# Masked row maximum with the half maxima in SBUF and eleven feed-forward blocks, in a two-stage attention kernel

## What is computed

```python
# attention stage: 16 heads of 16 channels
q = (x @ Wq.T + bq).reshape(B, S, H, D)          # k and v likewise, v with its bias bv
scores = einsum('bqnd,bknd->bnqk', q, k) / sqrt(D)
attn = softmax(scores, axis=1)                    # over the 16 heads n
out = einsum('bnqk,bknd->bqnd', attn, v)
return out.reshape(B, S, E) @ Wo.T + bo           # then x + this, layer norm
# layer stage, twice: window attention (8 heads of 64), then
h = layernorm(shift_token(x)) @ w1 + b1           # w1: 256 x 1364, HID = 682
a, g = split(h, 2, axis=-1)
x = x + (a * gelu(g)) @ w2 + b2                   # w2: 682 x 256
```

## Time and profile before

| | before |
|---|---|
| median of 3 runs | 4322.89 us (4319.83 to 4324.39) |
| the profiled execution | 4329.71 us, its span 4327.9 us |
| attention stage (first to last L409) | 63.6 to 1482.5 us of the span |
| layer stage (from the first projection) | about 1525 to 4328 us |
| PE, DVE, ACT, POOL busy | 92%, 71%, 66%, 51% of the span |
| DMA queues | under 20% of 16 engines |

### The profile page before, as it was taken

How to read it: one execution, slowest core, us unless ns; L and a number is a source line. 1 busy time by engine, 2 the same in 40 slices (tenths; PEclk the granted TensorE clock), 3 DMA queues, 4 the chain that set the end, 5 groups by cost and what they waited for, 6 DMA issues and landing times.

```text
span 4327.9 us, 96690 instructions
## 1 busy us (share of the span) xinstructions
PE 4001.2 (92%) x36356; PEld 3306.8 (76%) x36416; DVE 3055.6 (71%) x7412; ACT 2852.8 (66%) x7273; POOL 2198.8 (51%) x2168
## 2 busy tenths in 40 slices
PE   5999999999999769999999999999999999999997
PEld 3777777777777557888888888877888888888886
DVE  3888888888888756666666666666667666666664
ACT  3666666666666456677676767766766676666665
POOL 3888888988888823333333333333333333333332
PEclk8999999999999989999999999999999999999999
DMA  5453444434444010000000000000000000000000
GB/s 103 69 74 63 60 69 70 68 63 66 68 70 59 28 45 12 20 16 16 19 17 14 17 19 16 16 27 13 26 21 21 27 21 21 22 26 24 19 24 24
DMA packets 175047, 159.22 MB, mean 37 GB/s; under 512 B 22175, under 2 KB 173558, under 8 KB 174582
## 3 DMA queue, kind: packets, MB, share of 16 engines
q1 hardware_dynamic: 174582, 153.04, 19.1%
HBM read 52.31 MB, written 25.17 MB: 18 GB/s over the span
## 4 chain that ended last, share of the span: by engine, by line
PE 16%; issue 15%; ACT 15%; DVE 14%; POOL 5%; SPq 0%; DMA 0%; POOLq 0%; DVEq 0%; ACTq 0%
PE b_X L1439 4%; PE b_S L1459 3%; DVE b_S L1251 3%; PE b_M L1561 3%; ACT b_p L1199 3%; ACT b_hn L1083 2%; ACT L1167 2%; PE b_M L1552 2%; DVE b_ss L1225 2%; DVE b_qT L1240 2%; ACT b_g L1167 2%; DVE b_kT L1240 2%; POOL b_rstd L1041 1%; PE b_F L1588 1%; PE b_S L1469 1%
## 5 line engine op out<-in xcount | busy, mean ns | idle before, releaser
L251 POOL TENSOR_TENSOR a_z<-a_p 128x1024 f32<-128x1024 f32 x256 | 604.0, 2359 | 187.4 <-ACT a_p L338 184.9
L1199 ACT ACTIVATE b_p<-b_S,b_nb 128x256 f32<-128x256 f32 (+1 forms) x1024 | 444.5, 446 | 328.8 <-DVE b_nb L1251 328.8
L338 ACT ACTIVATE a_p<-a_S 128x512 f32<-128x512 f32 x1024 | 528.7, 602 | 191.3 <-PE a_S L528 189.5
L1439 PE MATMUL b_X<-b_wqkv,b_hT 128*128 128x512 f32 x2304 | 651.5, 419 | 1.3 <-DVE b_hT L1275 1.3
L1508 PE MATMUL b_F<-b_hnT,b_w 128*114 128x256 f32 (+1 forms) x4608 | 628.8, 286 | 5.7 <-issue 5.7
L1508 PEld LDWEIGHTS b_F<-b_hnT,b_w 128*114 128x114 f32 (+1 forms) x4608 | 573.6, 177 | 19.0 <-issue 6.1
L1439 PEld LDWEIGHTS b_X<-b_wqkv,b_hT 128*128 128x128 f32 x2304 | 418.1, 190 | 101.2 <-issue 21.8
L977 POOL TENSOR_TENSOR b_t<-b_t 128x512 f32<-128x512 f32 x128 | 165.1, 1290 | 633.8 <-DVE b_t L1223 633.8
L422 DVE TENSOR_TENSOR a_p<-a_p,a_O 128x1536 f32<-128x1536 f32 x256 | 447.2, 1747 | 5.4 <-ACT a_O L315 3.8
L1588 PE MATMUL b_F<-w_w,b_a 114*128 114x256 f32 (+1 forms) x1536 | 365.4, 388 | 69.4 <-DVE b_a L879 68.8
L1260 DVE TENSOR_SCALAR b_a<-b_F,w_b 114x256 f32<-114x256 f32 (+1 forms) x384 | 183.8, 479 | 340.9 <-ACT b_g L1110 340.8
(11 more groups left out here) (152 smaller groups left out, 8719.7 us busy)
## 6 DMA issues: line engine op xcount, KB each, us to landing
a_q<-a_parts SPq DMA_DIRECT2D x256, 128.0 KB, 5.0
a_k<-a_parts SPq DMA_DIRECT2D x256, 128.0 KB, 5.0
a_x<-in_x SPq DMA_DIRECT2D x16, 512.0 KB, 3.9
a_xr<-in_x SPq DMA_DIRECT2D x64, 128.0 KB, 5.2
x_after_heads<-a_n SPq DMA_DIRECT2D x64, 128.0 KB, 5.4
b_x<-x_after_heads SPq DMA_DIRECT2D x16, 512.0 KB, 4.1
x_after_layer<-b_xo SPq DMA_DIRECT2D x32, 256.0 KB, 2.8
b_x<-x_after_layer SPq DMA_DIRECT2D x16, 512.0 KB, 4.1
```

What stands on the lines that cost most here:

```text
L251: nc.gpsimd.tensor_tensor(z8[:], e[:, 0:8], e[:, 8:16], ALU.add).then_inc(s_zt, 1)
L338: nc.scalar.activation(probs[u % NE][:, hs], S[:, hs], ACT.Exp, scale=HDIM ** -0.5).then_inc(s_exp, 1)
L1199: last = nc.scalar.activation(probs[hf][:, i, keys(w_)], SB[:, i, keys(w_)], ACT.Exp, bias=nb[hf][:, i:i + 1], scale=-1.0, accum_out=rs[w_ ...
L1439: last = nc.tensor.matmul(X[i][:], hT_of(k, a), wqkv[:, b, k, i * INNER:(i + 1) * INNER], start=(k == 0 and (a, b) == PART_PAIRS[0]), stop ...
```

## The change

In the attention stage:

- The second half maximum goes to SBUF, into `half_max[:, 1]` beside the first, instead of `HM` in PSUM. Its waits for `s_lz` and `s_Y` are gone. The minimum now has both its inputs in SBUF.
- The first part of `sum_z` stands before bank 0 instead of before bank 1, and `output` after `times_v` and its neighbours instead of before.
- V's bias comes from a matmul of three bf16 rows into the bank (one of 512 columns for each two tiles), and V is moved to SBUF by ScalarE with plain copies at the end of units 14 and 15, instead of by VectorE.

In the layer stage:

- Chunks are 128 columns wide, five full and one of 42. The last chunk's value and gate columns stand in one block of 106 (values in columns 0 to 41, gates from 64), so there are 11 blocks, 66 matmuls in a pair of tiles.
- w2 and b2 come from the host as one array padded with zero rows to 6 x 128, in one DMA instead of three; all six L1588 chunks take 128 rows. The scale rows `srow` share the memory of `t2[0]`.

The diff's core:

```diff
-    Z, HM = YZ[:, 1, :P], YZ[:, 1, P:]
+    Z = YZ[:, 1, :P]
...
-                    nc.vector.tensor_reduce(out=low_max[:], in_=S[:, 0:8].rearrange("p h q -> p q h"),
-                                            axis=AX.X, op=ALU.max, negate=True).then_inc(s_hm, 1)
...
-                    if exists(nz):
-                        dve.wait_ge(s_lz, UNITS * nz + uz + 1)
-                    ny, _, uy = lagged(n, u, 5, UNITS)
-                    if uy % TILES == TILES - 1 and exists(ny):
-                        dve.wait_ge(s_Y, TILES * ny + uy // TILES + 1)
-                    dve.wait_ge(s_S, 2 * U + 2)
-                    nc.vector.tensor_reduce(out=HM, in_=S[:, 8:16].rearrange("p h q -> p q h"),
-                                            axis=AX.X, op=ALU.max, negate=True).then_inc(s_hm, 1)
+                    for half in range(2):
+                        dve.wait_ge(s_S, 2 * U + half + 1)
+                        nc.vector.tensor_reduce(out=half_max[:, half], in_=S[:, 8 * half:8 * half + 8].rearrange("p h q -> p q h"),
+                                                axis=AX.X, op=ALU.max, negate=True).then_inc(s_hm, 1)
                     dve.wait_ge(s_hm, 2 * U + 2)
                     need(dve, s_sub, 4 * U - 4)
-                    nc.vector.tensor_tensor(negmax[u % 2][:], low_max[:], HM, ALU.min).then_inc(s_nm, 1)
+                    nc.vector.tensor_tensor(negmax[u % 2][:], half_max[:, 0], half_max[:, 1], ALU.min).then_inc(s_nm, 1)
...
+                nc.tensor.matmul(B[j][:].rearrange("p (t c) -> p t c", t=2), ones_b[:],
+                                 b_rows[:, VALUE].unsqueeze(1).to_broadcast([3, 2, CH]), start=True, stop=False,
+                                 skip_group_check=True)
...
-            size = HC if c < CHUNKS - 1 else LAST
-            for part in range(2):
+            size = HC if c < CHUNKS - 1 else GATE_AT + LAST
+            for part in range(2 if c < CHUNKS - 1 else 1):
                 for k in range(CT):
-                    col = part * HID + c * HC
+                    col = part * FULL + c * HC if c < CHUNKS - 1 else 2 * FULL
```

More of the change, by code:

```diff
@@ L321, in _ @@
             part_of_qk(0, i, part)
+        act.wait_ge(s_pz, 3)
+        for j in range(2):
+            evacuate_v(0, 0, j)
         def normalise_rows(nn, qt):
@@ L575, in _ @@
                 project_v(0, tile, k)
-        pe.wait_ge(s_bor, 16 * 3)
         for b in range(4):
```

107 lines of the change are left out of this document (56 added, 51 removed).

## The result

The changed kernel takes 4288.26 us (median of 4 runs, 4285.34 to 4290.59) against 4323.08 (4319.83 to 4324.39) for the kernel before: a ratio of 0.992, with a 95% interval of 0.9903 to 0.9937. That is 35 us, or 0.8%, faster, where I had said 4304 and a range of 4258 to 4328.

The account below looks back on a forecast made before the run. It took attention's loop to close over exps, z8 and minimum, and layer tiles over a chain on engines other than TensorE. Terms 42 - 19 - 4.5 + 0 + 1, about 19 us, took the 4322.9 us median to 4304, range 4258 to 4328.

Parts of the forecast that it names:

- The wait for the output: Attention, output units: VectorE's second reduce no longer waits for the output projection; 0.65 us in each of 64, 42 us gained.
- The first sum moved: Attention: first sum of z ahead of bank 0 starts bank 1 0.12 to 0.22 us sooner, but counts nothing.
- the gain is swallowed whole: Attention: the moved sum's gain is lost because the minimum must wait for z8, which does not move.
- The lock term of 19 us: Attention: the minimum waits for GpSimd's z8 at the SBUF port; 0.11 us in each of 11 ordinary units, 19 us lost.
- z4 first: Attention: GpSimd's z4 precedes the minimum every time, 1.5 us a unit, about 4550 us; within the GpSimd-pace rival, chance 0.12.
- The minimum with two SBUF inputs: Attention: it waits for z8 and ends some 0.15 us after it, 0.4 to 0.8 us long; 19 us lost in all.
- The rival of no lock: Attention: port does not matter for so short an instruction; 26 us gained instead of 19 lost, 4259 us; chance 0.10.
- V's bias and move: Attention, units 12 and 14: two more matmuls per sequence, 0.3 us on the path, 4.5 us lost; ScalarE's copies cost nothing.
- The feed-forward blocks: Layer stage: six matmuls fewer save TensorE 0.70 us a pair, but it only waits longer before the scores; 0 us.
- one wait of 1.05: Layer stage, odd tiles: TensorE's wait before the scores grows from 0.35 to about 1.05 us.
- The loads: Ahead of the layer stage's first x: two DMA issues fewer, 1 us gained.
- The sum: Whole kernel: 42 - 19 - 4.5 + 0 + 1, about 19 us gained, median 4304 us, 0.44% faster.

Follow-up runs that it names:

- experiment 4: Changed kernel with the first sum of z back behind bank 0's scores, as before the change: 4331.45 us, ratio 1.0024 to the kernel before.
- experiment 5: Kernel of experiment 4 with one added wait: in unit 8 GpSimd's z4 waits for VectorE's minimum: 4315.76 us, ratio 0.9983 to the kernel before.
- experiment 1: Changed kernel with the minimum as a tensor_reduce over half_max, one SBUF input instead of two: 4256.02 us, ratio 0.9848 to the kernel before.
- experiments 1, 2 and 5: The second of these: kernel before with only both half maxima moved to SBUF, waits and order kept: 4371.59 us, ratio 1.0113.
- experiment 8: Changed kernel with twelve feed-forward blocks, the last chunk's second block of 106 columns and its gate read from partitions 64 to 105: 4293.85 us, ratio 0.9934.
- Experiment 10: Changed kernel with the second weights loaded in three transfers (114 partitions, 14 partitions, sixth block) instead of one of 128: 4296.7 us, ratio 0.9938.

## Why the prediction came out as it did

*The wait for the output.* Right in kind, its size too small. I gave an output unit 5.75 us (5.5 in unit 15), and it took 5.43 to 5.45: by the medians a sequence gains 3.84 us, not 2.7, and the kernel 61 us, not 42. The terms of the sum were too long. From `less_max` to the less-part, with both sums and all scores between, I had 1.86 + 1.26 = 3.12 us, and it is 2.96 (879.63 to 882.59); the output is 1.15, not 1.18. For `times_v` I took the middle of 1.01 and 1.24, and it took 1.01 (882.90 to 883.91). That is 0.16 + 0.03 + 0.13 (with the rounding up to 5.75), the whole difference of 0.32. The times from the earlier trace rows had switches between sums and scores in them, and that these go away when the first sum stands ahead of all scores is my reading; the late weights of the upper end did not come. My 42 us was also 2 us off my own terms: 25.5 - 22.75 is 2.75 us in a sequence, 44 in all.

*The first sum moved, "the gain is swallowed whole".* True of nine of the eleven ordinary units, which are 5.37 to 5.47 us without it and 5.37 to 5.45 with it (experiment 4). False of the kernel: the move is worth 43 us where I had none, and without it the changed kernel would take 4331 us, 8 more than the kernel before. This is the step that failed. The lock term of 19 us holds only while the minimum starts ahead of z4. I priced the rival "z4 first" as one that strikes all units or none, and gave it its chance on the evidence of one pair of rows; what decides it is who starts first, in each unit anew, and in unit 8 GpSimd comes 0.23 us behind the minimum with the sum moved, and 0.08 ahead of it without. That one unit is worth 16 us (experiment 5) to 23. So that the forecast's sign came out is in part luck: it hung on a part of the change that I had put at nothing.

*The minimum with two SBUF inputs.* Right: 0.65 us at the median, its end 0.15 us after z8's, ordinary units at 5.36 to 5.39 us. They lose 1.45 us in a sequence, 23 us in all, where I had 1.2 and 19. The rival of no lock fell with experiment 1; against a minimum with one SBUF input the lock costs 32 us, and that with a minimum that is 0.14 us slower by itself.

The Trainium skill's page "SBUF — State Buffer", section "Who interferes with whom", on which a sentence of the prediction drew, has the rule of experiments 1, 2 and 5: two SBUF inputs contend with a GpSimd instruction that reads SBUF, one doesn't, and whoever starts first holds the port for its whole instruction. The runs agree (0.42 us without exception with one input; 0.29 with two and z4 held back; 1.33 with z4 first).

*V's bias and move.* Unit 14 is 0.12 us longer, 2 us in all, and unit 13 is with the ordinary ones, 0.22 longer; I had 4.5 us for both, within its bounds of 0 to 9.

*The feed-forward blocks.* Right that the matmuls bring nothing, and for the reason given. From the second weights' matmuls behind the odd tile to the next scores I count 7.75 us in the earlier trace rows (3018.55 to 3026.30), and now 8.56 (2973.53 to 2982.09):

```profile
2973.53 2.75 PE L1582 MATMUL b_F<-w_w,b_a 128*128 128x256 f32 x12
...
2980.20 0.44 PE L1416 MATMUL b_X<-c_ident,b_hn 128*128 128x128 f32 x2 [0.32 <-ACT b_hn L1077]
...
2982.09 0.98 PE L1454 MATMUL b_S<-b_kT,b_qT 64*128 64x256 f32 x12 [0.43 <-DVE b_kT L1235]
```

Those 0.81 us are the 0.70 saved and 0.11 on top. They don't stand in one wait of 1.05, as I had written, but in a new one for the layer norm, in a longer one for the key copy and in small gaps between. The 0.11 is what I missed: the gate is now read from partitions 64 to 105, VectorE's wait for it went from 2.86 to 2.98, and the stage lost some 8 us (2711.4 to 2719.6 by the means of experiment 8) where I had 0.

*The loads.* I allowed 1 us for two issues fewer. The stretch between the stages takes 47.6 to 49.5 us in the three traces with transfers of 114 partitions against 43.1 to 44.5 in the eleven without, 4.5 us by the means. The first `less_max` comes at 62.4 to 63.9 us against 57.5 to 62.8, 3 us by the means, but the two ranges overlap, so that this part is not shown. Experiment 10 measures 8 for both. I had counted issues; the one issue that is slow and x's later landing are what I missed.

*The sum.* -61, +23 and +2 are -36 in attention by the medians of the middle sequences; the stage shows -31.5, with the first and the last sequence in it. With the loads at -8 and the layer stage at +8 that is about -32, against 35 measured by the medians; the other 3 us I can't place. Term by term, my 19 was too small by the output units (19 us), the loads (7) and V (2.5), and too large by the ordinary units (4) and the gate (8). Errors of both signs cancelled in part, so that the forecast came nearer than its terms did.

## What to carry to other kernels

A short VectorE instruction with two SBUF inputs on the loop that sets the pace should lose one of them wherever GpSimd is busy: one input in PSUM, or a reduce over a pair, even one that is 0.14 us slower by itself. Where that can't be done, look in the trace at who starts first, since a shift of 0.3 us ahead of it can cost the wait for a whole GpSimd instruction (experiment 4); an added wait that fixes the order can be a gain. And when work is taken from an engine that waits, look first at what the change does to the engine that is waited for: here six matmuls saved cost one ScalarE instruction its overlap, and the stage got longer.
